# Attention steps in another order: self-attention by query half, the third chunk's norm and queries in the last block, cross-attention slots laid out by hand

## What is computed

```python
x = x + L0_xattn(ln(x), ctx)   # causal self-attention, 16 heads of 16; cross-attention to 77
                               # context rows; FFN 256 -> 1024 -> 256; each with add and layernorm
x = x + L0_ffn(ln(x))          # one linear layer whose weight gets a low-rank addition
x = x + L1_xattn(ln(x), ctx)   # masked attention to the 77 context rows
x = x + L1_ffn(x)              # gated experts: causal attention of 8 mixed projections, then 8 MLPs
```

## Time and profile before

| | us |
|---|---|
| median of 3 runs | 1379.08 (1377.55 to 1393.95) |
| profiled execution | 1377.67 |
| its span, first to last instruction | 1375.9 |
| PE busy | 1206.2 (88%) |
| DVE busy | 849.1 (62%) |
| ACT busy | 562.1 (41%) |
| POOL busy | 312.1 (23%) |

### The profile page before, as it was taken

How to read it: one execution, slowest core, us unless ns; L and a number is a source line. 1 busy time by engine, 2 the same in 40 slices (tenths; PEclk the granted TensorE clock), 3 DMA queues, 4 the chain that set the end, 5 groups by cost and what they waited for, 6 DMA issues and landing times. The chain is left out here.

```text
span 1375.9 us, 19970 instructions
## 1 busy us (share of the span) xinstructions
PE 1206.2 (88%) x7150; PEld 847.5 (62%) x7150; DVE 849.1 (62%) x1814; ACT 562.1 (41%) x1201; POOL 312.1 (23%) x490
## 2 busy tenths in 40 slices
PE   7988999887887787999888876999999788899999
PEld 3543333332333335677667765899977667788898
DVE  4577776766555384566567786666644455865555
ACT  5215666555564355455225533210013333543332
POOL 5012222222220035544117652000010110600000
PEclk8999999999997899999979977999989999899999
DMA  5840363330441802000002000000030000000000
GB/s 192 184 116 2 55 61 48 47 48 1 71 71 43 145 7 58 1 1 1 1 20 103 2 0 1 1 1 1 1 123 0 0 1 0 1 0 16 16 17 16
DMA packets 37969, 50.71 MB, mean 37 GB/s; under 512 B 11098, under 2 KB 28784, under 8 KB 37232
## 3 DMA queue, kind: packets, MB, share of 16 engines
q1 hardware_dynamic: 37872, 49.44, 17.3%
HBM read 37.26 MB, written 11.77 MB: 36 GB/s over the span
## 5 line engine op out<-in xcount | busy, mean ns | idle before, releaser
L532 PE MATMUL PS<-ARENA 128*17 128x512 f32 (+14 forms) x2208 | 401.9, 419 | 67.1 <-ACT ARENA L1367 17.1
L532 PEld LDWEIGHTS PS<-ARENA 128*17 128x17 f32 (+5 forms) x2208 | 163.0, 127 | 239.0 <-issue 110.3
L1282 ACT ACTIVATE ARENA<-PS 128x512 f32<-128x512 f32 (+3 forms) x384 | 172.9, 490 | 143.8 <-PE PS L532 141.1
L1671 DVE TENSOR_REDUCE ARENA<-PS 128x1 f32<-128x128 f32 (+7 forms) x256 | 181.4, 751 | 66.1 <-PE PS L532 64.9
L532 PE MATMUL PS<-WQKVP,TRR 128*128 128x384 f32 x512 | 134.3, 344 | 1.5 <-ACT BC L1218 1.0
L2119 POOL TENSOR_SCALAR_AFFINE_SELECT ARENA<-ARENA 128x128 f32<-128x128 f32 x256 | 74.0, 296 | 219.0 <-ACT ARENA L1282 216.3
L532 PEld LDWEIGHTS PS<-W2P,INT 128*128 128x128 f32 x768 | 94.9, 188 | 2.8
L532 PE MATMUL PS<-W2P,INT 128*128 128x256 f32 x768 | 95.5, 279 | 0.0
L532 PEld LDWEIGHTS PS<-WQKVP,TRR 128*128 128x128 f32 x512 | 93.4, 192 | 2.6 <-ACT BC L1218 1.9
L1963 DVE SCALAR_TENSOR_TENSOR ARENA<-PS,rw,ARENA 128x384 f32<-128x384 f32 x112 | 69.2, 618 | 40.2 <-PE PS L532 39.5
L2091 POOL TENSOR_TENSOR rstd<-var,halves 128x4 f32<-128x4 f32 x36 | 38.1, 1058 | 245.8 <-DVE var L1516 197.7
(11 more groups left out here) (221 smaller groups left out, 1955.6 us busy)
## 6 DMA issues: line engine op xcount, KB each, us to landing
ARENA<-qk_parts SPq DMA_DIRECT2D x96, 128.0 KB, 5.6
qk_parts<-ARENA SPq DMA_DIRECT2D x8, 768.0 KB, 3.3
ARENA<-xq_parts SPq DMA_DIRECT2D x48, 128.0 KB, 6.0
ARENA<-in_w SPq DMA_DIRECT2D x2, 2048.0 KB, 10.7
xq_parts<-ARENA SPq DMA_DIRECT2D x8, 384.0 KB, 2.3
ARENA<-in_wqkv SPq DMA_DIRECT2D x1, 3072.0 KB, 10.0
X<-in_x SPq DMA_DIRECT2D x4, 512.0 KB, 7.1
ARENA<-in_wf SPq DMA_DIRECT2D x2, 1024.0 KB, 6.2
```

Of the source, the lines that this page charges most:

```text
L532: return nc.tensor.matmul(o, lhsT, rhs, start=start, stop=stop, **kw)
L1282: ins = nc.scalar.activation(PROB[GRP * (step % 2) + j][:, 0:w], PS[:, uses[key][0], 0:w], ACT.Exp, scale=HD ** -0.5)
L1671: ins = v.tensor_reduce(negm[:, n % 2, TPB * j + st:TPB * j + st + 1], PS[:, bank:bank + 2, :].rearrange("p b s -> p (b s)")[:, 0:P * (st ...
```

## The change

- `STEPS` runs through all key tiles of the first query half, then of the second, in place of alternating. For the last group the two halves are evacuated and turned apart (`evach`, `outh`): the first half in the last block, at units 20 and 23.
- With it, chunk 2's `norm` (from unit 25), `turn` (43) and both `xq` (45, 47) move into the last block. The last group's second half is turned in the first slot of the cross-attention.
- In a cross-attention step, `xpv` stands behind the second score (before: the third), `xout` behind the third (before: ahead of the second), and ACT copies the values ahead of the fourth exponential (before: after it).
- The lists `early` and `lately` are replaced by a table of slots. POOL's split of the first matrix moves from behind `xneg` 3 to slots of step 11; the transposes, evacuations and lower parts of FFN chunk 0 (`ffn_in`) move to slots of steps 12 and 13, in buffers that are free by then.
- `busy` matmuls go: 2 in each `xpv`, 8 and 4 at chunks 2 and 3 (64 in all), and 14 of the 20 ahead of the FFN.
- SP's stream is unchanged.

```diff
-STEPS = [(tt, c) for tt in range(TPB) for c in range(2) if tt < 4 * (c + 1)]
+STEPS = [(tt, c) for c in range(2) for tt in range(4 * (c + 1))]
...
+            if n == GROUPS:
+                if u == 20:
+                    yield "evach", n - 1, 0
+                if u == 23:
+                    yield "outh", n - 1, 0
+                if u >= 25 and u % 2 == 1 and u < 25 + 2 * NORM_PIECES:
+                    yield "norm", 2, u // 2 - 12
+                if u == 43:
+                    yield "turn", 2
+                if u in (45, 47):
+                    yield "xq", 2, u // 2 - 22
...
-    yield "evac", GROUPS - 1
-    yield "out", GROUPS - 1
+    yield "evach", GROUPS - 1, 1
     yield "xneg", 1
     yield from cross_plan()
...
     for t in range(XSTEPS):
         for j in range(GRP):
-            if j == 1 and t >= 2:
+            if j == 3 and t > 0:
+                yield "xevac", t - 1
+            yield "xscore", t, j
+            if j == 1 and t > 0:
+                yield "xpv", t - 1
+            if j == 2 and t >= 2:
                 yield from out(t - 2)
-            yield "xscore", t, j
-            if j == 2 and t > 0:
-                yield "xpv", t - 1
             yield "slot", t, j
-        if t > 0:
-            yield "xevac", t - 1
     yield from out(XSTEPS - 2)
     yield "xpv", XSTEPS - 1
     yield "xevac", XSTEPS - 1
     yield from out(XSTEPS - 1)
...
+def cross_slots():
+
+
+    slots = {}
+
+    def put(t, j, *op):
+        slots.setdefault((t, j), []).append(op)
+
+    put(0, 0, "outh", GROUPS - 1, 1)
+    for g in range(2):
+        put(0, 1 + g, "xqm", 2, g)
+    for piece in range(NORM_PIECES):
+        put((piece + 3) // 4, (piece + 3) % 4, "norm", 3, piece)
+    put(3, 0, "turn", 3)
+    put(3, 2, "xq", 3, 0)
+    put(3, 3, "xq", 3, 1)
+    put(4, 1, "xqm", 3, 0)
+    put(4, 2, "xqm", 3, 1)
+    for m, (t, j) in enumerate(((3, 1), (3, 2), (4, 0), (4, 3), (5, 0), (5, 1), (5, 2), (5, 3))):
+        put(t, j, "xmax", 2, m % 4, m // 4)
+    put(6, 0, "xneg", 2)
+    for piece, (t, j) in enumerate(((6, 2), (6, 3), (7, 0), (7, 1), (7, 2))):
+        put(t, j, "g2", 0, piece + 1)
+    for m, (t, j) in enumerate(((8, 2), (8, 3), (9, 0), (9, 1), (9, 2), (9, 3), (10, 0), (10, 1))):
+        put(t, j, "xmax", 3, m % 4, m // 4)
+    put(10, 2, "xneg", 3)
+    for piece, (t, j) in enumerate(((10, 3), (11, 0), (11, 1), (11, 2), (11, 3))):
+        put(t, j, "g2", 1, piece + 1)
+    for m, (t, j) in enumerate(((11, 0), (11, 1), (11, 2), (11, 3))):
+        put(t, j, "wf1", m)
+    for step, (t, j) in enumerate(((11, 3), (12, 2), (13, 2))):
+        put(t, j, "rank", step)
+    for m, (t, j) in enumerate(((12, 1), (12, 3), (13, 1), (13, 3))):
+        put(t, j, "ffn_in", m)
+    for piece, (t, j) in enumerate(((14, 0), (14, 1), (14, 3), (15, 0), (15, 1))):
+        put(t, j, "g2", 2, piece + 1)
+    return slots
...
-    late = [[("xqm", 2, g)] for g in range(2)]
-    inputs = chunk_inputs(3)
-    early = chunk_inputs(2) + inputs[:2] + late + inputs[2:]
-    late = [[("xqm", 3, g)] for g in range(2)]
-    maxima = chunk_maxima(2)
-    early += maxima[:2] + late + maxima[2:] + [[("xneg", 2)]]
-    lately = chunk_maxima(3) + [[("xneg", 3)], [("rank", 0)]]
-    lately += [[("g2", 0, piece)] for piece in range(1, G2_PIECES)] + [[("rank", 1)]]
-    lately += [[("g2", 1, piece)] for piece in range(1, G2_PIECES)] + [[("rank", 2)]]
-    lately += [[("g2", 2, piece)] for piece in range(1, G2_PIECES)]
+    slots = cross_slots()
     for op, *at in cross_steps():
-        if op != "slot":
+        if op == "slot":
+            yield from slots.get(tuple(at), [])
+        else:
             yield (op, *at)
-            if op == "xscore" and at == [8, 0]:
-                while early:
-                    yield from early.pop(0)
-        else:
-            t, j = at
-            if t < 8:
-                if early and t < 7:
-                    yield from early.pop(0)
-                if early and t >= 5:
-                    yield from early.pop(0)
-                if t == 7:
-                    while early:
-                        yield from early.pop(0)
-            else:
-                if lately and not (lately[0][0][:2] == ("g2", 2) and t < 14):
-                    yield from lately.pop(0)
-    while lately:
-        yield from lately.pop(0)
...
-        TRG = [nc.alloc_sbuf_tensor_at(f"TRG{s}", [P, KC, 512], F32R, offset=w6_at + 4096 * s)[:, :, :] for s in range(2)]
-        TRGF = region(13376, 1024, "p (i k s) -> p i k s", i=4, k=KC)
+        TRG = [nc.alloc_sbuf_tensor_at(f"TRG{s}", [P, KC, 512], F32R, offset=w6_at + 4 * at)[:, :, :] for s, at in enumerate((1248, 0))]
+        TRGF = [region(lo, 1024, "p (i k s) -> p i k s", i=4, k=KC) for lo in (27904, 13376, 13376, 13376)]
...
+                        if n < GROUPS - 1:
+                            claim(("values", n), [6, 7], signals=0)
+                        else:
+                            for half in range(2):
+                                claim(("values", n, half), [6 + half], signals=0)
...
-                        busy(4 if n >= 2 else 0, first)
...
-                        busy(8 if c >= 2 else 0, bank)
...
-                    busy(2, bank)
...
+                elif op == "ffn_in":
+                    i = n
+                    first = wide(1)
+                    claim(("t_g2", i), [first])
+                    normalized(pe, "g2", i)
+                    for k in range(KC):
+                        ins = nc.tensor.transpose(PS[:, first, P * k:P * k + P], H[:, i, P * k:P * k + P], ident[:, :])
+                    filled(ins, ("t_g2", i))
...
-            pe.wait_ge(wf1_split, 4)
-            turn("t_g2", "g2", H, 0)
             for s in range(6):
                 if s < 4:
                     if s == 0:
                         claim(("idle", 2), [2], 0, 0)
-                        busy(20, 2)
+                        busy(6, 2)
+                        pe.wait_ge(wf1_split, 4)
...
+            def evacuate_part(c, i):
+
+                key = ("t_g2", i)
+                arrived(act, key)
+                if c > 1:
+                    act.wait_ge(trg_ready, 4 * c)
+                src = PS[:, uses[key][0], 0:D].rearrange("p (k s) -> p k s", k=KC)
+                nc.scalar.copy(TRR[:, :, P * i:P * i + P], src)
+                released(nc.scalar.copy(TRGF[c][:, i % 4], src), key)
...
+                    act.wait_ge(pv_done, len(STEPS) * n + (4, len(STEPS))[half])
+                    arrived(act, ("out", n - 1))
+                    released(nc.scalar.copy(OTS[:, 512 * half:512 * half + 512], PS[:, 6 + half, :]), ("values", n, half))
...
-                    if n % 2 == 0 and at[0] == 0:
-                        drained(dve, ("out", GROUPS // 2 * (n // 2 + 1) - 1))
+                    if n == 0 and at[0] == 0:
+                        drained(dve, ("out", GROUPS // 2 - 1))
+                    if n >= 2 and at[0] == 0:
+                        drained(dve, ("out", GROUPS - 1, n - 2))
...
-                    elif op == "xneg" and n == 3:
-
-                        loaded(pool, "wf1")
-                        for m in range(4):
-                            cols = slice(m * FF // 4, (m + 1) * FF // 4)
-                            split(WF1[:, :, cols], WF1P[0][:, :, cols], WF1P[1][:, :, cols], wf1_split)
+                    elif op == "wf1":
+                        if n == 0:
+                            loaded(pool, "wf1")
+                        cols = slice(n * FF // 4, (n + 1) * FF // 4)
+                        split(WF1[:, :, cols], WF1P[0][:, :, cols], WF1P[1][:, :, cols], wf1_split)
+                    elif op == "ffn_in":
+                        lower_part(0, n)
                     elif op == "g2" and at[0] == 1:
...
-                    lower_parts(0)
```

More of the change, by code:

```diff
@@ L831, in _ @@
                     filled(ins, ("out", n))
+                elif op == "outh":
+                    half = at[0]
+                    drained(pe, ("values", n, half))
+                    first = wide(1)
+                    claim(("out", n, half), [first])
+                    for i in range(4):
+                        ins = nc.tensor.transpose(PS[:, first, P * i:P * i + P],
+                                                  OTS[:, 512 * half + P * i:512 * half + P * i + P], ident[:, :])
+                    filled(ins, ("out", n, half))
+                elif op == "ffn_in":
+                    i = n
+                    first = wide(1)
+                    claim(("t_g2", i), [first])
[3 more added lines that the diff above has]
+                    filled(ins, ("t_g2", i))
             def cross():
@@ L1331, in _ @@
                     else:
-                        arrived(act, ("out", GROUPS - 1))
+                        arrived(act, ("out", GROUPS - 1, n))
                     released(nc.scalar.copy(XOUT[n % 2], PS[:, 6, :]), key)
@@ L1404, in _ @@
                 if s < 3:
-                    evacuate_parts(s + 1)
```

(4 more changed lines are left out.)

43 lines of the change are left out of this document (23 added, 20 removed).

## The result

The changed kernel takes **1370.56 us** (median of 11 executions, 1362.32 to 1374.35), the kernel before 1378.97 (11 executions, 1373.03 to 1393.95): ratio 0.9933, 95% interval 0.9907 to 0.9958. It is faster by 0.7%, a quarter of the 36 us that I forecast, and outside my range of 1322 to 1364. Single executions of one kernel scatter by 3 to 7 us (standard deviation). Ratios and their intervals leave out the executions that took over 1.5% longer than the fastest one of their kernel, medians do not.

A forecast was written before the change was run, and what follows sets the result against it. The cross-attention was taken as the weak stretch, bound by a ring in which PE and ACT wait for each other, plus waits. Terms 0 - 4 + 5 - 30 - 6.3 = -35.3 gave 1343 us as a median, range 1322 to 1364.

The forecast's parts named there:

- The cross-attention: Whole cross-attention: from 111.2 us to 75, plus 6 for low-clock stretches, so -30, ends -38 and -18.
- the ring: Cross-attention step, where PE and ACT wait for each other: 3.1 us for 4.0 in the new order.
- rival (c): Cross-attention steps stay at 4.0 us because another wait takes its place: 1353 us; chance 0.12.
- Rival (a): Cross-attention without idle matmuls falls to the low clock, steps about 4.5 us: 1362 us; chance 0.12.
- The waits: PE waits in the cross-attention: 6 us at the first score of chunk 2, 3 at chunk 3's.
- rival (b): SP's stores and loads of chunks 2 and 3 each end 5 us later, lengthening waits: 1353 us; chance 0.18.
- Steps by half: Self-attention blocks 1 to 8: order of the load matters little, 0; ends -1 and +1.5 us a block.
- The slower rival: Diagonal tiles in a row make value products wait behind POOL, then low clock: 55 us, 1398; chance 0.05.
- Blocks 5 and 6: Blocks with the norm of chunks 0 and 1: nobody waits for POOL, 2 us back each, -4; ends 0, -8.
- The last block: Last self-attention block takes on chunk 2's norm, transposes, turn and two `xq`: +5 us, ends +2 and +9.
- The FFN: Last transposes to second FFN matrix: POOL decides, 17.4 us for 23.7, so -6.3; ends -4 and -7.5.
- Rival (e): New order does nothing outside the end, since the waits only move: 1372 us; chance 0.03.

The follow-up runs named there:

- experiment 6: Kernel before with only the order inside a cross-attention step as changed, all idle matmuls kept: 1380.95 us, ratio 0.9999.
- all_fixes: Changed kernel with alternating order in the first seven groups, all 78 idle matmuls back, DVE's weight split earlier and POOL's later: 1355.01 us, ratio 0.9833.
- experiment 10: Repairs combined on the changed kernel: four together 1355.01 us; with chunk 2's rows ahead of chunk 3's loads 1358.92; that without the alternating order 1362.65.
- experiment 5: Kernel before with only the 78 idle matmuls taken out: median 1390.65 us for 1380.55; ratio 0.9954 from five of twelve executions.
- idle_all: Changed kernel with all 78 idle matmuls put back: 1361.53 us, ratio 0.9865.
- experiment 4: Changed kernel with idle matmuls put back: all 78, 1361.53 us, ratio 0.9865; only the 46 at the waits and ahead of the FFN, 1364.17, ratio 0.9901.
- experiment 9: Changed kernel with SP issuing chunk 2's rows ahead of the loads of chunk 3's queries: 1366.8 us, ratio 0.9913.
- experiment 1: Kernel before with only the list of steps changed, to run by query half: 1385.19 us, ratio 1.0045.
- experiment 3: Changed kernel with more row maxima in the narrow steps and fewer in the wide ones: 1373.0 us, ratio 0.997.
- experiment 7: Changed kernel with DVE's second-matrix split ahead of the norm's scaling: 1366.04 us; separately, with POOL's first-matrix split behind the lower parts: 1365.16 us.

## Why the prediction was wrong

The direction was right and the chance of 0.35 on "same" took in the result; the size was off by 27 us. These steps of the sum failed, or held.

**The cross-attention, -30 forecast.** The step was right: 3.1 to 3.5 us at full clock, and the ring does not stay at 4.0 (rival (c) falls, experiment 6). What failed is the line "I add 6 us for low-clock stretches". I weighed the clock by how dense PE's work is in one undisturbed step and found it "no higher than the new one's"; that was no evidence on a stretch with holes, in which the matmuls I saw taken out were the filling. **Rival (a) was the right mechanism**, and 0.12 far too little for it. Its price for a step at the low level, about 4.5 us, is that of step 14, 4.46 us from first exponential to first exponential. From T, the end of the last self-attention product (422.4), the first exponential stands at T + 0.7 (forecast 1.2), the turn at T + 12.5 (13), step 5 at T + 25.9 (24), chunk 2's first score at T + 43.5 (41), chunk 3's at T + 66.2 (59.5), the last transposes at T + 92.2 (75, with the reserve 81). The last part alone is 26.0 for 15.5, and at full clock it is 17.9 in `all_fixes` (491.27 to the last transposes at 509.16). So some 8 of the 11.8 us missed are the clock in that part. That it is 1.2 GHz which makes it long is shown by the same part at either level (experiment 10); that the missing matmuls let the clock fall, by the 17 traces (experiment 5). What they cost in time is shown less surely: the medians say 9 us, and one trace of `idle_all` has the stretch no shorter. The first two parts ran at 0.77; what of their 7 us above my count is clock and what is DVE's queue is not separated.

The Trainium skill (TensorE: Matmul & The Clock Gate, What's actually happening) takes the throttled state for the default, which activity releases. Experiments 4 and 5 agree in both directions: the mean clock goes from 0.928 to 0.947 with the matmuls back, and from 0.938 to 0.920 with them out.

**The waits.** I had 6 and 3 us; they were 3.57 and 2.89, each with SP's chain as I laid it out. The first is a matter of the execution: over the six traces with SP's stream and the waits unchanged and no idle matmuls it runs from 2.5 to 7.1 us. Of rival (b) this much is so: both first scores came later than counted, by 2.5 and 7 us, but PE came later as well, so that the waits did not grow. Taking chunk 2's rows from behind the twelve loads moved the wait more than it saved in the trace (experiment 9).

**Steps by half, 0 forecast with +1.5 as the bound per block.** It came to +1.35, near the bound, all of it inside the sum's -8 to +12. "Two blocks with quite different loads take 36.0 and 35.9, so the order of the load matters little" is the failed step: those differ in DVE's load, and here it is PE's own work in the wide steps that fills them (experiments 1 and 3). The slower rival had neither the place nor the mechanism: its tiles (1, 0) to (3, 0) take 9.1 us in all for 9.0, and what got longer are (1, 1) to (3, 1), without more waiting for clears.

**Blocks 5 and 6, -4 forecast.** They came to -1.5 and -1.4 against before. PE's waits for POOL's clears in them fell from 5.8 to 1.6 us, those for DVE's maxima rose from 3.3 to 6.7. Against a plain block of the new order they cost 4.0 and 2.9 for 6.9 and 5.6, so my 2 back in each was low, and the 1.35 of the order hides it. The two are not cleanly apart: with the order alone block 6 was no shorter (experiment 1).

**The last block, +5 forecast.** By the ends of the last product it takes 41.45 us for 35.83: +5.6, close to the forecast.

**The FFN, -6.3 forecast.** It came to -1.5. "POOL, not PE, decides" failed: in the new order POOL starts earlier and meets DVE's split, which then runs at POOL's pace and becomes the bound. I had costed that split at nothing without naming its cover, which was that POOL stood still for most of it. With the split moved it is 18.4 for the 17.4 forecast (experiment 7). The Trainium skill (SBUF — State Buffer, Who interferes with whom) says that DVE and GpSimd share a port pair as an exclusive lock, that the one first there keeps it for the instruction and that the issue order decides. The rows agree in both directions: 1.43 us for four casts ahead of POOL and 5.80 behind it, and for POOL's first instruction 2.49 us behind DVE's subtractions in the kernel before, for 1.28.

Rival (e), that the new order does nothing outside the end, comes nearest in number (1372), by luck: what happened are large moves of both signs, and its gain at the end did not come.

## What to carry to other kernels

Matmuls without a result are work for the clock: before taking them out, or before shortening a step in which they stand, read the granted clock of the whole stretch with its holes, and price the stretch at the low level as the likely case if it has waits. When a stage is brought forward, list what ran in its shadow on the other engines; where DVE's work met POOL's here, the one that came second waited. And a shorter step is worth nothing where the stretch waits for something else: time the ring alone and the waits alone before adding their gains.

## What the runs showed of the hardware

- Time and granted clock go together over the executions of one and the same kernel: the kernel before ran from 1367.2 us at 0.950 to 1394.8 at 0.925, without its idle matmuls from 1360.9 at 0.941 to 1400.0 at 0.908.
- Six DMAs of 8 KB land 7.6 us after issue behind twelve loads of 128 KB in SP's queue, and 1.9 us with the queue empty.
- DVE's casts, and its subtractions of two SBUF inputs, behind POOL subtractions of 128x512: 0.36 us becomes 1.45 for a cast, 0.62 becomes 1.42 or 1.73 for a subtraction (a quarter of the rows above). POOL's own go from 1.28 to 1.46 (11.64 / 8) and 1.54, and the one that came behind DVE took 2.49.
- Over the same 128 us the granted clock is 0.85 to 0.95 in the seven traces with all 78 idle matmuls and 0.72 to 0.80 in the nine without them.
